# First attention: GpSimd's tiles of distances laid out with four neighbouring distances side by side

## Time and profile before

| | us |
|---|---|
| median of 3 runs | 2874.37 (2874.24 to 2877.35) |
| the profiled execution, its own time | 2873.56 |
| its span in the trace | 2871.8 |
| first to last tile of the first attention (GpSimd, line 828) | 30.0 to 566.4 |
| gelus of phases 3 to 5 start at | 242.3, 309.4, 376.5 |

### The profile page before, as it was taken

How to read it: one execution, slowest core, us unless ns; L and a number is a source line. 1 busy time by engine, 2 the same in 40 slices (tenths; PEclk the granted TensorE clock), 3 DMA queues, 4 the chain that set the end, 5 groups by cost and what they waited for, 6 DMA issues and landing times. The chain is left out here.

```text
span 2871.8 us, 46605 instructions
## 1 busy us (share of the span) xinstructions
PE 2351.9 (82%) x19181; PEld 976.2 (34%) x19181; DVE 2200.5 (77%) x3034; ACT 1938.1 (67%) x2018; POOL 1076.5 (37%) x409
## 2 busy tenths in 40 slices
PE   4677777788756766786899888998779979999996
PEld 1122222255212222244333243333454533333334
DVE  5788888867999999985798807997450268899984
ACT  5999999922733333344699847997632269999981
POOL 6999999812089999932000400004010000000000
PEclk8999999979878889897999999999989989999998
DMA  2012111110144444302301010001010030210000
GB/s 77 1 45 59 61 58 45 45 55 9 29 154 161 166 163 154 118 9 62 66 12 29 18 37 1 13 13 46 11 42 0 5 99 16 42 32 21 16 8 28
DMA packets 66719, 145.50 MB, mean 51 GB/s; under 512 B 13235, under 2 KB 29983, under 8 KB 65792
## 3 DMA queue, kind: packets, MB, share of 16 engines
q1 hardware_dynamic: 66496, 142.40, 16.9%
HBM read 117.92 MB, written 24.25 MB: 50 GB/s over the span
## 5 line engine op out<-in xcount | busy, mean ns | idle before, releaser
L828 POOL TENSOR_TENSOR l0a_diff_pool<-l0a_A,l0a_a_of_t 128x2048 f32<-128x2048 f32 x128 | 531.6, 4209 | 30.4 <-ACT l0a_a_of_t L843 29.2
L2121 ACT ACTIVATE l2x_pT<-ps 128x1024 f32<-128x1024 f32 x512 | 470.2, 1167 | 13.9 <-PE ps L2079 13.9
L2272 ACT ACTIVATE l3he_pT<-ps 128x1024 f32<-128x1024 f32 x480 | 445.2, 1063 | 17.0 <-PE ps L2207 17.0
L1438 PE MATMUL ps<-l1s_hc,all_ident 128*128 128x512 f32 x512 | 283.8, 707 | 156.5 <-POOL l1s_hc L1409 102.3
L774 DVE SCALAR_TENSOR_TENSOR l0a_diff_dve<-l0a_A,l0a_pos,ps 128x512 f32<-128x512 f32 x512 | 344.9, 742 | 30.4 <-PE ps L619 30.3
L1400 POOL TENSOR_TENSOR l1s_dBx<-l1a_dtx,l1a_Bs 128x1024 f32<-128x1024 f32 x128 | 297.4, 2351 | 109.4 <-POOLq L1134 109.4
L1424 ACT ACTIVATE ps<-l1a_dt,l1a_A 128x1024 f32<-128x1024 f32 x128 | 143.1, 1118 | 268.2 <-DVE l1s_hc L1483 215.9
L2207 PE MATMUL ps<-l3h_Qs,l3h_Ks 75*32 75x512 bf16 x4096 | 274.9, 383 | 10.1 <-DVE ps L2277 10.1
L2079 PE MATMUL ps<-l2m_Qs,l2m_Ks 75*32 75x512 bf16 x4096 | 274.4, 387 | 9.8 <-PEq L2534 9.8
L2094 PE MATMUL ps<-l2x_pT,l2m_Va 128*9 128x512 f32 x2048 | 271.0, 602 | 11.4 <-DVE l2s_oT L2654 6.1
L2676 POOL TENSOR_TENSOR l2s_E<-l2s_E,l2x_rest 128x2048 f32<-128x2048 f32 x16 | 73.1, 4571 | 496.6 <-DVEq L2399 491.5
(11 more groups left out here) (493 smaller groups left out, 3689.6 us busy)
## 6 DMA issues: line engine op xcount, KB each, us to landing
l1a_Bs<-l1a_bc SPq DMA_DIRECT2D x64, 512.0 KB, 3.6
l1s_Cs<-l1a_bc SPq DMA_DIRECT2D x64, 512.0 KB, 4.6
l0a_band_rows<-l0a_band SPq DMA_DIRECT2D x32, 512.0 KB, 4.9
l0a_band<-l0a_exps SPq DMA_DIRECT2D x14, 512.0 KB, 5.1
l2m_Ks<-l2m_parts SPq DMA_DIRECT2D x36, 128.0 KB
l2m_Qs<-l2m_parts SPq DMA_DIRECT2D x72, 64.0 KB
l3h_Qs<-l3h_parts SPq DMA_DIRECT2D x72, 64.0 KB
l0a_band<-l0a_zero SPq DMA_DIRECT2D x8, 512.0 KB, 7.4
```

What stands on the lines that cost most here:

```text
L828: pool.tensor_tensor(out, window(s), atb[:, p % 2, :].unsqueeze(1).broadcast_to([P, 4, CH]), ALU.subtract).then_inc(diff_pool, 1)
L1438: mm = pe.matmul(g.ps[:, (4 + 2 * h + q) * CH:(5 + 2 * h + q) * CH], g.ident[:, :], hc[:, m % NHC, q * CH:(q + 1) * CH], start=(n == 0), s ...
L2121: act.activation(pT[:, turn % NPT, :], g.ps[:, slot * QC:(slot + 1) * QC], ACT.Exp).then_inc(expd, 1)
L2272: act.activation(pT[:, (4 * m + j) % NPT, :], g.ps[:, slot(turn)], ACT.Exp).then_inc(expd, 1)
```

## The change

GpSimd's tiles and VectorE's tiles now hold four neighbouring distances, 16 dg + 4n + c. GpSimd writes its tile as 512 times of 4 distances (c innermost), reading A as overlapping runs of four neighbours, with A(t) repeated four times by a step of 0. ScalarE goes over the same 2048 columns as before. TensorE reads GpSimd's tiles through `by_distance`: 512 columns at a step of four elements (16 bytes); VectorE's tiles stay as they were. Rows of the PSUM bank are then no longer in the order of distances, so the transpose of the logits becomes a product with a permuted unit matrix `by_row`, made once in the setup.

```diff
+        by_row = r.sb("distance_of_row", [P, P])
...
+                    dve.tensor_copy(by_row[:, :].rearrange("p (n c h) -> p c n h", n=4, c=4), g.ident[:, :].rearrange("p (c n h) -> p c n h", c=4, n=4))
...
         def window(s):
             p, q, hf, dg, k, n = place(s)
-            first = A[:, hf, k, q * CH + 16 * dg + n + 1:q * CH + 16 * dg + n + 2]
-            return bass.AP(first.tensor, first.offset, [list(first.ap[0]), [4, 4], [1, CH]])
+            first = A[:, hf, k, q * CH + 16 * dg + 4 * n + 1:q * CH + 16 * dg + 4 * n + 2]
+            return bass.AP(first.tensor, first.offset, [list(first.ap[0]), [1, 4], [1, CH]])
+
+        def by_distance(tile, s):
+            if s % TPG in D_AT:
+                return tile
+            return tile.rearrange("p c t -> p (c t)").rearrange("p (t c) -> p c t", c=4)
...
-                        mm = pe.transpose(out[:, dg * P:(dg + 1) * P], L[:, p % 2 * GPP + dg, b * P:(b + 1) * P], g.ident[:, :])
+                        mm = pe.matmul(out[:, dg * P:(dg + 1) * P], L[:, p % 2 * GPP + dg, b * P:(b + 1) * P], by_row[:, :], start=True, stop=True)
...
-                    ge, _, _ = slot(s)
+                    ge = by_distance(slot(s)[0], s)
...
-                        d = 16 * dg + 4 * c + n
+                        d = 16 * dg + 4 * n + c
...
-                    pool.tensor_tensor(out, window(s), atb[:, p % 2, :].unsqueeze(1).broadcast_to([P, 4, CH]),
-                                       ALU.subtract).then_inc(diff_pool, 1)
+                    pool.tensor_tensor(out.rearrange("p c t -> p (c t)").rearrange("p (t c) -> p t c", c=4), window(s).rearrange("p c t -> p t c"),
+                                       atb[:, p % 2, :].unsqueeze(2).broadcast_to([P, CH, 4]), ALU.subtract).then_inc(diff_pool, 1)
```

## The result

| | before | changed |
|---|---|---|
| median of 4 runs | 2875.10 us (2874.24 to 2877.35) | 2895.72 us (2893.84 to 2899.90) |
| profiled execution, own time | 2873.56 | 2894.99 |
| first layer in the trace | 610.0 | 633.3 |

The ratio is 1.0072, with an interval of 1.0056 to 1.0088: 20.6 us slower. So the change lives in the first attention alone, as the prediction had it.

A forecast was written before the change was run, and what follows sets the result against it. In full phases, GpSimd's path and one through TensorE's lag and VectorE were taken to meet in slot 15. GpSimd -6.9, logits' product +4.3 and TensorE's reads +8 gave +5.4 on 2873.56: 2879 us, range 2861 to 2925.

The forecast's parts named there:

- a wait of 1 to 3 us in slot 15 behind line 774 and full phases of 68 to 69 us: Signs named for the forecast: ScalarE waiting 1 to 3 us in slot 15; phases 2 to 7 at 68 to 69 us.
- GpSimd's tiles: GpSimd's subtraction at 3.8 us for every tile, bounds 3.77 and 4.5; 6.9 us less, from phases 0 and 1.
- Rivals 3: Runs of four cost GpSimd its pace: 2916 at the slow pace, 2952 with an overhead per run; chance 0.22.
- rival 4: GpSimd's tiles mix both paces to 4.14 us, nothing won, TensorE's price stays: 2886; chance 0.18 together with rival 5.
- Two paths meet in slot 15: Full phases: GpSimd's path and TensorE's lag plus VectorE's 12.55 us meet; removing GpSimd's wait moves ScalarE's four slots on.
- Rival 2: The path through slot 15 has unseen slack, so ScalarE's waits go: 2856, or 2862 with half TensorE's price; chance 0.18.
- The logits' product: Four true products on TensorE take 0.36 us more than transposes; logits 0.72 us later in six phases: 4.3 us more.
- those of slots 5 and 6 stand ahead of slot 7's reduction: On a late TensorE, the logits' products of slots 5 and 6 precede slot 7's reduction, making the logits 0.72 us later.
- TensorE's reads: TensorE's reduction of GpSimd tiles at a 16-byte step costs 0.45 us more per tile; 8 us more over six phases.
- rival 5: TensorE takes double for strided tiles, 19 us more in place of 8: 2890; chance 0.18 together with rival 4.
- rival 1: GpSimd fast and TensorE's strided reads free: 2871, no change; chance 0.14.
- slots 1, 2 and 3 carry it to slot 7: TensorE, behind from slot 1, carries three tiles' added 0.45 us to slot 7 in six phases: 8 us.

The follow-up runs named there:

- e1: The changed kernel, but TensorE reads GpSimd's tiles side by side as before (values altered); 2871.83 us, 0.9995 of the kernel before.
- e4: Not a version: GpSimd's sixteen tiles of a phase made in sixteen forms of the subtraction to time them (values altered); ran once, 2875.75 us.
- e5: The changed kernel, but GpSimd's tile holds pairs of neighbouring distances, so TensorE reads at a step of 8 bytes; 2874.03 us, 0.9996 of the kernel before.
- f1: The kernel before, plus a second copy of A(t) two columns later in memory for GpSimd's tiles n=0 and n=3; 2868.86 us, ratio 0.9978.
- f2: As f1, with VectorE subtracting the maxima in slots 12, 13, 14 and 16 in place of 13 to 16; 2864.02 us, 0.9961 of the kernel before.
- f3: The kernel before, with only the maxima moved to slots 12, 13, 14 and 16; 2873.98 us, ratio 0.9996.
- e2: The changed kernel, but the logits go through the one-instruction transpose again (values altered), strided read kept; 2890.18 us, 1.0047 of the kernel before.

## Why the prediction was right, and which steps failed

The direction and the range held (2861 to 2925, slower at 0.51). That says less than it seems to: the range is 64 us wide and the chance of the direction was near even. The loss was forecast at 5.4 us and came as 20.6, and the signs that were named for the forecast, a wait of 1 to 3 us in slot 15 behind line 774 and full phases of 68 to 69 us, weren't there: the changed kernel waits 4.08 us for TensorE in slot 14 and has phases of 72.1. They came in e1, where the strided read is away. So the number, 2879, was 17 us short, and by its own steps:

- **GpSimd's tiles**: 3.6 us, under the 3.77 that I took as the lower bound. That bound rested on "both operands are still read 2048 times", and no run shows how a held operand is read. In e4 even two plain reads of a tensor (3599 ns) lie under it, and a held operand against a plain one (3855) above it, so the reason given for 3.8, that A(t) changes a quarter as often, isn't borne out either. The gain from phases 0 and 1 was forecast at 6.9 and came as 5.9. e1, whose TensorE isn't late, has 7.0. The term came out near although the pace did not: where GpSimd keeps ahead of ScalarE anyway, a still faster tile wins little. Rivals 3 and 4 fell; a pace between the two, as rival 4 had it, shows only in e4's runs of four against a plain operand (4251).
- **Two paths meet in slot 15**: right. e1, e5 and f1 give ScalarE a fast GpSimd and find it waiting for VectorE (18.7, 19.3, 15.6 us); f2 against f1 and f3 shows the pair. Rival 2 fell with it: there was no slack. In the changed kernel itself TensorE's lateness covers this meeting.
- **The logits' product**: forecast 4.3; 5.4 without strided reads (e1), 8.2 beside them (e2). The duration was a little short (0.5 us more per four, not 0.36); beside strided reads the step that failed is "those of slots 5 and 6 stand ahead of slot 7's reduction": that counted to the wrong waiter. With a late TensorE all four stand ahead of slot 14's tanh.
- **TensorE's reads**: the main miss. "I take 0.45, the nearest row" was a weight load; the stream pays 0.92, the doubling that I had priced as rival 5 at 2890, and rival 1, strided reads for nothing, fell. Nor is it clear that the row's 198 against 140 ns was the price of the step: loads of 128 side-by-side columns for a product took 192 ns in the same trace (line 540, below). By rival 5's sum the forecast would have been 5 to 6 us short. The remainder is "slots 1, 2 and 3 carry it to slot 7": three tiles a phase, where eight strided tiles stand ahead of the second tanh. The tanh of slots 6 and 14, which needs only GpSimd's tiles reduced, stood in the description and in no step of the sum.

```profile
L540 PEld LDWEIGHTS ps<-l0a_wv,all_hT x62: 186/192/192, 77.5 to 482.4; 128*128 128x128 f32 x62
```

TensorE's work up to slot 11 closes the sum, at a granted clock of 1.00 in both traces. From the first gelu of phase 4 to the second tanh were 27.55 us before (309.39 to 336.94); TensorE ended slot 11 at 334.54 after 1.61 us of idle time, so its work alone needed 23.5. Eight tiles at 0.92 and four products at 0.5 add 9.4, which makes 32.9; the changed kernel shows 32.67 (313.28 to 345.95), 5.1 more than before, and its full phases are 5.0 longer (72.1 against 67.1). In phases 0 and 1, which have few or no products with the values, the tanhs wait 0.97 and 0.26 us: there even 1.98 us of reduction are nearly hidden, as the prediction said of 1.45.

Of the two rules that the prediction weighed: the Trainium skill, "Advanced Engine Details and Errata", section "Memory Cachelines", asks for at least two hits on a line of 16 bytes and announces a penalty for a new line with every access. The runs agree: one access in 16 bytes takes TensorE's stream from 593 to 1077 ns, two from 617 to 636, though they can't tell that rule from one on the length of the step. The Trainium skill, "GPSIMD Engine Reference", section "Elementwise — side-by-side cycle accounting", has a floor of about 2.6 cycles per element for two inputs (the 2.5 that the prediction worked with, for 4.27 us, stands in the page's section on dispatch). By an estimate from the page's 2.6 a tile would take 4.44 us. The measurement decides against either: 3.60 us.

## What to carry to other kernels

Before an engine is made faster, find the second path that ends in the same waits and relieve it in the same edit; here a fast GpSimd alone and another order of the maxima alone were worth nothing in a full phase, both together 0.6 us of 67.1, and with a better order 1.9. When a producer's layout is changed, price the consumer that reads it most often (each GpSimd tile is written once and streamed by TensorE twice), keep two neighbouring fp32 side by side in what TensorE streams (the step of 8 bytes cost 3%, that of 16 doubled it), and follow each engine that becomes late to every instruction that waits for it, not only to the one that was late before. A two-operand GpSimd instruction is worth trying with one operand shifted by two columns.

## What the runs showed of the hardware that I had not expected

- GpSimd's fp32 subtraction of 128x2048 has two paces, 3.81 and 4.59 us, set by the difference of the two operands' columns modulo 4 (e4, f1). The layouts of fours and of pairs, in which an element of A(t) is held for four or two reads, give 3.60 and 3.66, but a held operand against a plain one 3.86. Why a plain tensor against itself is also at 3.60, with a difference of 0, is open: there both operands read the same addresses.
- TensorE's reduction of a tile read at a step of 16 bytes takes 2.01 us at a granted clock of 0.50 and 1.98 at 1.00; side by side it takes 1.93 and 1.06. What the step costs is a matter of the full clock.
- A VectorE `tensor_scalar` from SBUF to SBUF took up to 8.63 us beside GpSimd's subtractions, 0.49 without them, and 0.75 read from PSUM. The Trainium skill, "SBUF — State Buffer", section "Who interferes with whom", has an exclusive lock on a pair of ports that VectorE, in its two-port modes, which `tensor_scalar` can enter, shares with GpSimd; whoever issues first has it for the whole instruction. The trace agrees in kind, though no run here shows the mode, and the wait lasted longer than one GpSimd instruction: it spans two whole ones.
